# K, the probabilities and x turned by DMA in a pipelined attention and feed-forward kernel

## The reference

```
x  = L0_attn_x                        # [4, 512, 1024] f32, 2048 tokens
xn = layernorm(x)
q, k, v = xn@Wq.T+bq, xn@Wk.T+bk, xn@Wv.T+bv        # 32 heads of 32, per token
scores = einsum('bshd,bsgd->bshg', q, k) / sqrt(32)  # heads against heads of one token
attn   = softmax(where(scores > 0.001, scores, -inf))
attn_out = einsum('bshg,bsgd->bshd', attn, v) @ Wo.T + bo
ffn_out  = (silu(xn@Wg.T) * (xn@Wu.T)) @ Wd.T        # int4 values with group scales, 3584 wide
out = x + attn_out + ffn_out
```

## Time and profile before

| what | value |
|---|---|
| median of 3 runs | 2207.54 us (2207.36 to 2208.41) |
| profiled execution | 2210.67 us, its span 2208.9 us |
| TensorE busy | 2100.9 us, 95% |
| DVE, ACT, GpSimd busy | 1664.8, 1374.9, 1361.2 us |
| attention loop, tiles 1 to 15 | about 71 to 763 us of the span |
| last attention tile (i = 16) | about 764 to 853 us |
| one steady tile | 46.5 us |

### The profile page before, as it was taken

The page is one execution under the profiler, slowest core; times in us unless marked ns, Lnnn a source line. Parts: engine busy times, 40 slices in busy tenths (PEclk is TensorE's granted clock), DMA queues, the critical chain, the costliest instruction groups (busy, mean ns, idle before and its releaser), DMA issues. The chain is left out here.

```text
span 2208.9 us, 39955 instructions
## 1 busy us (share of the span) xinstructions
PE 2100.9 (95%) x12032; PEld 1041.6 (47%) x12032; DVE 1664.8 (75%) x1904; ACT 1374.9 (62%) x2353; POOL 1361.2 (62%) x785
## 2 busy tenths in 40 slices
PE   7999999999999899989999999999999999999996
PEld 5555555555555554433444444444444444444444
DVE  5576667766676631049989989998998999999896
ACT  4687787887878743124565566656656665665653
POOL 1345435444445401005888888888888888888886
PEclk9999999999999999999999999999999999999998
DMA  8001000001001133412212211221221122122118
GB/s 286 30 30 40 36 28 34 32 28 47 28 28 38 68 105 113 160 34 67 57 47 52 70 44 47 66 57 47 60 64 43 47 66 57 47 66 57 43 25 309
DMA packets 156187, 144.08 MB, mean 65 GB/s; under 512 B 101488, under 2 KB 130160, under 8 KB 156144
## 3 DMA queue, kind: packets, MB, share of 16 engines
q1 hardware_dynamic: 156144, 143.50, 21.4%
HBM read 96.29 MB, written 25.17 MB: 55 GB/s over the span
## 5 line engine op out<-in xcount | busy, mean ns | idle before, releaser
L681 PE MATMUL banks<-xt,lower 128*128 128x512 f16 x3584 | 861.7, 379 | 29.9 <-ACT lower L935 16.3
L1253 POOL TENSOR_TENSOR acc<-acc,lower 128x1024 f32<-128x1024 f32 x327 | 772.1, 2365 | 176.2 <-ACT lower L962 176.2
L962 ACT ACTIVATE lower<-banks,down_scale 128x512 f32<-128x512 f32 x654 | 413.7, 683 | 356.5 <-PE banks L706 261.5
L1135 DVE SCALAR_TENSOR_TENSOR lower<-banks,gate_scale,lower 128x1024 f32<-128x1024 f32 x392 | 479.2, 1277 | 139.4 <-PE banks L681 133.5
L681 PEld LDWEIGHTS banks<-xt,lower 128*128 128x128 f16 x3584 | 337.4, 98 | 486.6 <-DVE lower L1135 80.2
L528 PE MATMUL banks<-wt,xt_tile 128*128 128x512 f16 x2304 | 552.7, 379 | 8.0 <-issue 4.1
L1135 DVE SCALAR_TENSOR_TENSOR lower<-banks,up_scale,lower 128x1024 f32<-128x1024 f32 x392 | 479.5, 1278 | 51.1 <-PE banks L681 44.9
L706 PE MATMUL banks<-lower 128*128 (+1 forms) x1792 | 459.8, 381 | 4.6 <-DMA lower<-lower 4.4
L1210 POOL TENSOR_TENSOR stacks<-unit,stacks 128x512 f16<-128x512 f32 x192 | 225.4, 1198 | 385.3 <-ACT stacks L807 385.3
L528 PEld LDWEIGHTS banks<-wt,xt_tile 128*128 (+1 forms) x2304 | 212.3, 98 | 205.0 <-issue 7.5
L706 PEld LDWEIGHTS banks<-lower 128*128 (+1 forms) x1792 | 175.7, 98 | 217.7 <-issue 18.5
(11 more groups left out here) (65 smaller groups left out, 1572.1 us busy)
## 6 DMA issues: line engine op xcount, KB each, us to landing
lower<-in_L_ffn_gate_q_dram SPq DMA_DIRECT2D x28, 512.0 KB, 3.7
lower<-in_L_ffn_up_q_dram SPq DMA_DIRECT2D x28, 512.0 KB, 4.4
lower<-in_L_ffn_down_q_dram SPq DMA_DIRECT2D x28, 512.0 KB, 3.9
x_tile<-in_L_attn_x_dram SPq DMA_DIRECT2D x16, 512.0 KB, 3.6
xt_scratch<-xt_tile SPq DMA_DIRECT2D x16, 512.0 KB, 2.7
ctx_scratch<-ctx_parts SPq DMA_DIRECT2D x16, 512.0 KB, 2.8
lower<-ctx_scratch SPq DMA_DIRECT2D x4, 2048.0 KB, 9.0
xt<-xt_scratch SPq DMA_DIRECT2D x4, 2048.0 KB, 16.3
```

Of the source, the lines that this page charges most:

```text
L681: last = mm(psum[:, 2 * (slot % 3) + c, :], gu_t[:, mat, g, :], xt[:, (2 * half + c) * CT:(2 * half + c + 1) * CT, part, g, :], start=(par ...
L962: run(down_tmp[:, buffer, c * BANK:(c + 1) * BANK], psum[:, 6 + c, :], ACT.Copy, scale=scale)\
L1135: v.scalar_tensor_tensor(out=acc_of[:, half, :], in0=gu_pair(slot % 3), scalar=scale[:, :, :].rearrange("p t k -> p (t k)")[:, bass.ds(t * ...
L1253: g.tensor_tensor(acc[:, half, ho, :], acc[:, half, ho, :], down_tmp[:, buffer, :], ALU.add).then_inc(down_added, 1)
```

## The change

- K and the probabilities are no longer turned by TensorE. SP issues DMA_TRANSPOSE from `stacks` (one DMA of 32 blocks, `turn_k`) and from `p_stack` (four DMAs of eight blocks, `turn_probs`), straight into `turned` and `probs_t`. In the table only Q (now R0 to R3, of tile i itself) and V (T4 to T7, of tile i-1) are left.
- x too: ACT and DVE write the parts of the still unturned `x_tile` into a new buffer `x_parts` (`x_part`), and SP turns both at once, 16 blocks (`turn_x`). In the opening these parts come ahead of the first weights in ACT's and DVE's lists.
- Tokens in a group of four are now neighbours (4g + r) for K and scores, so the scores' block is taken with a step of four columns. ctx gets another layout. ACT writes a product block's high part directly from PSUM into `ctx_parts` in four 32x256 pieces, DVE the low part behind it (`head_products_hi`, `head_products_lo`); `ctx_32` and GpSimd's part go.
- `STEPS` and the constants are rewritten; each tile's context is stored by SP two tiles later, in four DMAs.

```diff
-        STEPS = [["T0"], ["T1"], ["T2"], ["T3"], ["T4"], ["T5"], ["T6", "T7"], ["S0"], ["S1"], ["S2"],
...
+        STEPS = [["S0"], ["S1"], ["S2"], ["S3"], ["X", "T4"], ["T5"], ["T6"], ["T7"], [], [], [], [], ["R0"], ["R1"],
...
         def opening(weights, first_x, quarter, next_norm, next_x):
+            first_x()
             for w in range(4):
                 weights(w)
-            first_x()
             for w in range(4, 3 * KT):
                 weights(w)
                 quarter(w - 4)
                 if w == NEXT_NORM:
                     next_norm()
-            next_x()
+                if w == NEXT_NORM + 2:
+                    next_x()
             for s in range(3 * KT - 4, 3 * KT):
                 quarter(s)
@@ -271,6 +269,9 @@
...
+        def block_of(k, r):
+            src = pair(v_pair(k)).rearrange("p (g r a b) -> p r b a g", r=TG, a=KT, b=TG)
+            return src[r * DH:(r + 1) * DH, r, :, :, :]
+        def context_block(k, r, part):
+            return ctx_parts[r * DH:(r + 1) * DH, :, part, :, 8 * k:8 * k + 8]
...
+        k_turns = turned[:, K, :].rearrange("p (x t) -> p x t", t=P)
...
-            def turn_x(i):
-                pe.wait_ge(xn_ready, i + 1)
...
-                for k in range(KT):
-                    last = turn(x_pair(i)[:, k * P:(k + 1) * P], x_tile[:, k * P:(k + 1) * P], ident32[:])
-                last.then_inc(x_turned, 1)
...
             def project(i, s):
                 u, ks = s // 4, range(2 * (s % 4), 2 * (s % 4) + 2)
                 if s == 0:
-                    pe.wait_ge(x_lo, i + 1)
-                    pe.wait_ge(x_hi, i + 1)
+                    pe.wait_ge(x_turned, i * 16 + 16)
...
-                    pe.wait_ge(batch_out[0], j * 8 + 4)
-                    pe.wait_ge(batch_out[1], j * 8 + 4)
-                    wait_pos(pe, pv_out[0], j * 4)
-                    wait_pos(pe, pv_out[1], j * 4)
+                    pe.wait_ge(batch_out[0], j * 4 + 2)
+                    pe.wait_ge(batch_out[1], j * 4 + 2)
+                    pe.wait_ge(k_turned, j * 16 + 16)
+                    wait_pos(pe, ctx_lo, j * 4)
                 elif k >= 2:
                     pe.wait_ge(s_out, j * 4 + (k - 1))
                 for n in range(8):
                     at = (8 * k + n) * P
                     last = mm(pair(s_pair(k))[:, n * P:(n + 1) * P], turned[:, Q, at:at + P],
-                              turned[:, K, at:at + P], start=True, stop=True)
+                              k_turns[:, :, TG * (8 * k + n):TG * (8 * k + n + 1)], start=True, stop=True)
...
@@ -640,17 +599,21 @@
                         if s >= 2:
                             output_unit(s // 2 - 1, range(4 * (s % 2), 4 * (s % 2) + 4))
                     for kind, n in steps_of(i, s):
-                        if kind == "X":
-                            turn_x(i + 1)
...
             def x_part(i):
-                act.wait_ge(x_turned, i + 1)
-                wait_pos(act, xt_stored, i * 16 - 16)
-                wait_pos(act, unit_done, i * 6 - 6)
-                flat = xt_tile[:, :, :].rearrange("p a b -> p (a b)")
-                run(flat[:, bass.ds((i % 2) * (2 * KT * P), KT * P)], x_pair(i), ACT.Copy).then_inc(x_hi, 1)
+                act.wait_ge(xn_ready, i + 1)
+                wait_pos(act, x_turned, i * 16)
+                run(x_parts[:, HI, :], x_tile[:], ACT.Copy).then_inc(x_hi, 1)
...
+            def head_products_hi(j, k):
                 act.wait_ge(pv_done, j * 4 + (k + 1))
                 if k == 0:
-                    wait_pos(act, ctx_lo, j)
-                block_copies(j, k, (0, 1), lambda d, s: run(d, s, ACT.Copy), pv_out[0])
+                    wait_pos(act, ctx_stored, j * 64)
+                for r in range(TG):
+                    last = run(context_block(k, r, HI), block_of(k, r), ACT.Copy)
...
             def x_part(i):
-                flat = xt_tile[:, :, :].rearrange("p a b -> p (a b)")
                 dve.wait_ge(x_hi, i + 1)
-                v.tensor_tensor(flat[:, bass.ds((i % 2) * (2 * KT * P) + KT * P, KT * P)], x_pair(i),
-                                flat[:, bass.ds((i % 2) * (2 * KT * P), KT * P)], ALU.subtract).then_inc(x_lo, 1)
+                v.tensor_tensor(x_parts[:, LO, :], x_tile[:], x_parts[:, HI, :], ALU.subtract).then_inc(x_lo, 1)
...
+            def head_products_lo(j, k):
+                dve.wait_ge(ctx_hi, j * 4 + (k + 1))
+                for r in range(TG):
+                    last = v.tensor_tensor(context_block(k, r, LO), block_of(k, r), context_block(k, r, HI),
+                                           ALU.subtract)
+                last.then_inc(ctx_lo, 1)
...
-            def context_lo(j):
-                pool.wait_ge(ctx_hi, j + 1)
...
+                return xt_tile[:, :, :].rearrange("p a b -> p (a b)")[:, bass.ds((i % 2) * (2 * KT * P), 2 * KT * P)]
+            def turn_x(i):
                 sp.wait_ge(x_lo, i + 1)
                 anchor(sp)
-                src = xt_tile[:, :, :].rearrange("p a b -> p (a b)")[:, bass.ds((i % 2) * (2 * KT * P), 2 * KT * P)]
+                if not isinstance(i, int) or i > 1:
+                    sp.wait_ge(xt_stored, i * 16 - 16)
+                    anchor(sp)
+                    sp.wait_ge(unit_done, i * 6 - 6)
+                    anchor(sp)
+                sp.dma_start_transpose(xt_slot(i).rearrange("p (n t) -> p n t", t=P),
+                                       x_parts[:, :, :].rearrange("p a b -> p (a b)")).then_inc(x_turned, 16)
+            def store_xt(i):
+                sp.wait_ge(x_turned, i * 16 + 16)
+                anchor(sp)
+                src = xt_slot(i)
...
+            for w in range(4):
+                load_w(w)
+            turn_x(0)
+            for w in range(4, 8):
                 load_w(w)
             for dst, b in ((bias_qkv[:, 0, :], bq), (bias_qkv[:, 1, :], bk),
...
                 load_w(w)
                 if w == 12:
                     store_xt(0)
-                    load_x(1)
...
+            def turn_k(i):
+                if isinstance(i, int) and i == 0:
+                    sp.wait_ge(w_turned, 3 * KT)
+                sp.wait_ge(unit_lo, i * 6 + (2 * K + 2))
+                anchor(sp)
+                wait_pos(sp, s_done, i * 4)
+                anchor(sp)
+                sp.dma_start_transpose(k_turns, stacks[:, K, :, :].rearrange("p x c -> p (x c)"))\
+                    .then_inc(k_turned, 16)
+            def turn_probs(j, q):
+                sp.wait_ge(p_lo, j * 4 + (q + 1))
+                if q == 0:
+                    anchor(sp)
+                    wait_pos(sp, pv_done, j * 4)
+                anchor(sp)
+                at = slice(8 * q, 8 * q + 8)
+                sp.dma_start_transpose(probs_t[:, :].rearrange("p (g c) -> p g c", c=P)[:, at, :],
+                                       p_stack[:, at, :, :].rearrange("p g n h -> p (g n h)"))\
+                    .then_inc(p_turned[q], 16)
...
                 if not isinstance(i, int) or i + 1 < TT:
                     load_x(i + 1)
-                    store_xt(i + 1)
+                if not isinstance(i, int) or i > 1:
+                    store_context(i - 2)
+                if not isinstance(i, int) or i + 1 < TT:
+                    turn_x(i + 1)
                 if not projects(i):
                     for n in range(2, KT):
                         load_wo(n)
+                for q in range(4):
+                    turn_probs(i - 1, q)
+                if not isinstance(i, int) or i + 1 < TT:
+                    store_xt(i + 1)
+                if projects(i):
+                    turn_k(i)
+                if not projects(i):
```

206 lines of the change are left out of this document (89 added, 117 removed).

## The result

The changed kernel takes 2157.93 us in the median (2157.11 to 2159.74), the kernel before 2207.97: a ratio of 0.9774, 95% interval 0.9757 to 0.9791. That is 50 us faster. I had forecast 2191, that is 17 us, and a range of 2170 to 2218: the sign was right, the size wrong by a factor of three, the range too. The profiled execution took 2158.44 us for a span of 2156.5.

A forecast was written before the change was run, and what follows sets the result against it. TensorE bounds the attention stage, then a chain through ACT would: 13 tiles from 46.5 to 45.05 us (-18.9), opening +7.3, last tile -5, so 2210.7 - 16.6 - 3.1 = 2191 us; range 2170 to 2218.

The forecast's parts named there:

- Rival 4: Attention loop: TensorE bound by its issue, 38.2 us a tile plus 1.5 of starts; 2122 us in all; chance 0.03.
- Rival 1: Granted clock does not fall in the loop (8.5 us less), opening overlaps (up to 5 less): 2178 us; chance 0.17.
- The clock: Steady tile: granted clock halves behind TensorE's wait before R0, 1.65 us in four tiles of ten, 0.65 on average.
- The chain: Steady tile: copies, softmax and stacks on ACT, DVE and GpSimd delay R0 to 25.35 us; tile 44.4 before clock charge.
- starts after waits: Steady tile: 0.4 us added to TensorE's sum for starting again after waits.
- The end tiles of the loop: First and last of the 15 looped tiles: already some 2 us shorter than 46.5, so credited with no gain.
- The opening: Before the loop: +7.3 us, between +2 and +9, from later w rows, a lowered clock and four Q batches moved ahead.
- K's turn: DMA transpose of K, 32 blocks: lands 10.3 us after issue (bounds 6.5 and 12.4), hidden with 0.3 us to spare.
- the slower rival: Attention loop: K's transpose lands after 11.2 us and delays S0 in every tile; up to 2223 us; chance 0.13.
- The rate of the Trainium skill: Transposing DMAs at 350 to 400 GB/s; forecast used the trace's 219 instead, K's data 4.8 us rather than 2.8.
- The feed-forward stage: Stage after attention, from about 910 us on: untouched by the change, keeps its time.
- The last tile: Last attention tile: 12 batches fewer (-5.3 us) and +0.3 for later Wo rows and context; -5, between -7 and -2.

The follow-up runs named there:

- the kernel with the longer chain: Against the changed kernel: one more VectorE pass per tile, the row maximum taken again just before the reciprocals; 2178.20 us.

## Why the prediction was wrong

- **Stage and sign** were right: issue falls by 4.4 us, and a chain through ScalarE, VectorE and GpSimd takes part of it back, 1.0 us where I forecast 3.0 with the clock. Rival 4 (no chain) fell: dividing behind unit copy 1, without the collision, brought 1.4 us a tile, and moving the whole softmax and x's parts behind it 2.9. Rival 1 (no fall that costs, 2178) was nearest, and still 20 too high.
- **The clock, 0.65 a tile, 8.5 us in all: the step that failed in kind.** I charged it at R0 and wrote of T6 that the wait at R0 would take it back, which it did. But a wait of 2.25 at R0 was not there (1.25), the falls came at T6 (five of thirteen tiles), and there they are free. With the changed kernel's waits the right charge was 0. At R0, in the kernel with the longer chain, the price of the one fall was 1.59, against my 1.65.
- **The chain, 44.4 instead of 43.07, 17 us in all: the term that was mis-sized.** R0 came 24.62 after the tile's start instead of 25.35. The error grew along the chain: 0.1 at unit copy 5, 0.25 at the copy of T4, 0.55 at the division's end, 0.7 at GpSimd's. The largest piece, 0.3 of the 0.7, is the division, 1.54 in the earlier trace rows and 1.22 now: GpSimd's pair ran into its start then, until 380.64, and here GpSimd had gone idle (its row in the trace of before is below). The experiments show the same pass at 2.07 beside GpSimd's pair. To this I had added 0.4 "for starts after waits" and 0.1 of rounding, for which the trace has no counterpart. An error of 1.33 was nearly as large as the gain of 1.45 that I forecast for a tile.

```profile
377.85 2.79 POOL L1210 TENSOR_TENSOR stacks<-unit,stacks 128x512 f16<-128x512 f32 x2 [8.57 <-ACT stacks L807]
```

- **The end tiles of the loop, given nothing: 6.3 us.** They were 2.5 us shorter than a steady tile, and I took this for a sign that they had nothing to give. They lost as many batches and gained 2.7 and 3.6.
- **The opening** (+6.9 for +7.3) came from other parts than I named: the wait was for block 4 (4.13), not block 8, which starts 2.7 later without a wait, where I had 5.5 with the clock; the four Q batches and the wait before R2 made 3.9, where I had 2.7. The first quarter came 1.6 later, not within 1, since TensorE's list puts block 4's turn ahead of it. That the sum came out right is luck.
- **K's turn** landed after 6.7 us, near the lower bound of 6.5. I took 10.3, issue and data in series, because in the row of eight blocks data started at the issue's end, and this gave the slower rival 13%. The longer turns show that it was a coincidence: data starts 1.2 after the issue does, whether SyncE needs 1.24, 1.94 or 4.81 for it, and then runs at 212 to 217 GB/s. So 8, 16 and 32 blocks land after 3.1, 4.3 and 6.7, 0.15 us more a block, which is the time of its data at that rate. S0 had 3.1 to spare, not 0.3.
- **The rate of the Trainium skill** (Advanced Engine Details and Errata, X-Bar Transpose) is 350 to 400 GB/s. K's turn disagrees as the small ones did: its data ran at 217 GB/s, and at 207 to 220 in the kernel that turns K twice. With the page's rate the sum that fits here (1.2, the data, 0.5) would give a landing after some 4.5 us (an estimate), against 6.7 measured.
- **The feed-forward stage** gained 2.4 us that I did not forecast. It takes 1244.1 to 1245.0 in the thirteen traces that have the change; of the kernel before there is one trace, of an execution 2.7 us above the median of the others, so how much of the 2.4 belongs to that execution is open. (The stage begins at 962 in the kernel before, not at the 910 that I wrote; no sum used it.) The last tile was 1.5 better than forecast.
- **The range** failed with the sum: its lower end held one error at a time (the clock, or a chain shorter by 0.4). Chain, clock and end tiles missed in the same direction, 32 us together.

## What to carry over

Before charging a wait or a fallen clock, find the next wait behind it on the same engine. What is shorter than that costs nothing, as long as the work that ends that next wait does not itself start from the delayed part (at T6 it did not, at S0 it did); what stands after the last wait costs in full. A VectorE pass that reads two operands from SBUF has two prices in this kernel, with GpSimd busy beside it and without; take the one that holds in the new order, and bound the chain by the other. A tile whose bound is a chain is shortened by moving the step that joins it (here one unit copy before the softmax), not by removing work of the waiting engine in front of the wait.
